# First FFN's down product in four 32-row strips, with weights stationary and x1 kept feature-major

## The reference, cut to what matters

```python
# L0_cond: w = weights[itok_B_1_198];  einsum('bct,bcd->bdt', x, w)
gate_w = spline_reconstruct(gate_cp, 2048, 512)
up_w   = spline_reconstruct(up_cp, 2048, 512)
down_w = spline_reconstruct(down_cp, 512, 2048)
inter  = jax.nn.silu(einsum('bsh,ih->bsi', h, gate_w)) * einsum('bsh,ih->bsi', h, up_w)
ffn    = einsum('bsi,hi->bsh', inter, down_w)
x = x + ffn                                   # x1
x = x + _L1_ffn_ref(_L1_cond_ref(x, ...), ...)  # W + adapter, then router, top 2 of 8 experts
```

## Time and profile before

| | |
|---|---|
| runs before | 1277.27 us median of 3 (1273.51 to 1279.76) |
| profiled execution | span 1274.5 us, from the first to the last instruction; nothing of this execution outside its span was read, and the span is 2.8 us less than the median of the runs |
| busy in the span | TensorE 1161.4 us (91%), weight loads 1073.4 us (84%), VectorE 647.9 us (51%), ScalarE 476.7 us (37%), GpSimd 679.1 us (53%) |
| instructions | 29820 |

### The profile page before, as it was taken

How to read it: one execution, slowest core, us unless ns; L and a number is a source line. 1 busy time by engine, 2 the same in 40 slices (tenths; PEclk the granted TensorE clock), 3 DMA queues, 4 the chain that set the end, 5 groups by cost and what they waited for, 6 DMA issues and landing times. The chain is left out here.

```text
span 1274.5 us, 29820 instructions
## 1 busy us (share of the span) xinstructions
PE 1161.4 (91%) x9814; PEld 1073.4 (84%) x9815; DVE 647.9 (51%) x1223; ACT 476.7 (37%) x1023; POOL 679.1 (53%) x1035
## 2 busy tenths in 40 slices
PE   2579999999999999989999937999999999999995
PEld 1368899999999998878999936999998999899994
DVE  5867777767767677543444432333333333333332
ACT  2355656565666665532323201222222222222221
POOL 4856666666666666620434432555555545555553
PEclk9769999999999999997999967999999999999998
DMA  6044444445555555436736111475747474744443
GB/s 249 10 147 150 174 174 173 175 179 180 188 195 193 191 189 194 141 135 242 258 105 234 68 43 42 75 177 125 209 80 217 76 217 83 208 79 82 77 77 60
DMA packets 75085, 187.07 MB, mean 147 GB/s; under 512 B 12992, under 2 KB 26056, under 8 KB 70704
## 3 DMA queue, kind: packets, MB, share of 16 engines
q1 hardware_dynamic: 49904, 137.09, 30.6%
q0 software_dynamic: 19200, 38.94, 16.5%
q10 hardware_dynamic: 5952, 10.65, 2.3%
HBM read 114.76 MB, written 71.90 MB: 146 GB/s over the span
## 5 line engine op out<-in xcount | busy, mean ns | idle before, releaser
L880 POOL TENSOR_TENSOR in_lo<-inner,in_hi 128x512 fp32r<-128x512 f32 x128 | 168.6, 1317 | 133.4 <-ACT in_hi L1034 133.2
L1577 POOL TENSOR_TENSOR idle<-small 128x1 f32<-128x1 f32 x284 | 93.3, 331 | 196.7 <-DMA out<-result,scatter_at 123.9
L1655 PE MATMUL banks<-slots,zt_hi 128*128 x568 | 190.4, 335 | 4.9 <-DVE zt_lo L1744 2.9
L1657 PE MATMUL banks<-slots,zt_lo 128*128 x568 | 183.8, 324 | 0.0
L1656 PE MATMUL banks<-slots,zt_hi 128*128 x568 | 183.3, 323 | 0.0
L957 PE MATMUL banks<-down_hi,in_hi 64*128 64x320 f32 x1024 | 164.9, 308 | 0.0
L957 PE MATMUL banks<-down_lo,in_hi 64*128 64x320 f32 x1024 | 164.9, 307 | 0.0
L957 PE MATMUL banks<-down_hi,in_lo 64*128 64x320 f32 x1024 | 164.5, 307 | 0.0
L1756 DVE TENSOR_TENSOR hid<-silu_g,banks 128x352 f32<-128x352 f32 x71 | 37.0, 521 | 208.7 <-PE banks L1657 208.7
L1600 POOL DMA_INDIRECT out<-result,scatter_at x71 | 113.7, 1601 | 26.4 <-issue 22.7
L874 POOL TENSOR_TENSOR f_lo<-f_sum,f_hi 128x256 fp32r<-128x256 f32 x128 | 96.3, 769 | 37.8 <-ACT f_hi L1025 34.7
(11 more groups left out here) (221 smaller groups left out, 3055.9 us busy)
## 6 DMA issues: line engine op xcount, KB each, us to landing
gate_up_dram<-split_gu SPq DMA_DIRECT2D x16, 1408.0 KB, 4.9
slots<-gate_up_dram SPq DMA_DIRECT2D x16, 1408.0 KB, 6.8
expert_down_dram<-split_down SPq DMA_DIRECT2D x16, 768.0 KB, 7.1
slots<-expert_down_dram SPq DMA_DIRECT2D x16, 768.0 KB, 7.8
raw_gu<-in_expert_gu SPq DMA_DIRECT2D x16, 704.0 KB, 8.4
x_t<-in_x_t SPq DMA_DIRECT2D x16, 512.0 KB, 3.5
x_both<-in_x SPq DMA_DIRECT2D x16, 512.0 KB, 4.4
x_both<-in_x_res SPq DMA_DIRECT2D x16, 512.0 KB, 3.6
```

What stands on the lines that cost most here:

```text
L880: nc.gpsimd.tensor_tensor(in_lo[:, cs, :], inner[u % 2][:, :, :], in_hi[:, cs, :].bitcast(F32), ALU.subtract).then_inc(in_done, 1)
L1577: nc.gpsimd.tensor_tensor(idle[:, at:at + 1], small[:, 0:1], small[:, 0:1], ALU.add)
L1655: nc.tensor.matmul(psum[bank][:, 0:FD], zt_hi[:, k, :], w_high, start=(k == 0), stop=False)
L1657: ins = nc.tensor.matmul(psum[bank][:, 0:FD], zt_lo[:, k, :], w_high, start=False, stop=(k == DK - 1))
```

## The change

The hidden rows are sorted into 4 classes of 32 rows per group. `down` now takes the weights as the stationary operand (32 rows x 128 columns) and streams 256 tokens; its four classes stand in four 32-row strips of the array, each with a bank of its own. The moment weights become an operand of their own (`mom_w`, 128 columns that hold high and low parts), with two more matmuls. The output is feature-major, so nothing is transposed; `across` runs in three steps over running sums of neighbouring classes. The residual, x1 and its store are feature-major too, so `adapted_layer` loads x1 transposed (into a single buffer), takes high and low parts from SBUF, and makes the token rows of `out` by TensorE's transposes, a ScalarE copy and a store. `features` is 64-row pairs instead of full-array matmuls against a block-diagonal operand. `DOWN_AT` puts the eight `down` products of a tile into six visits. Three of the seven `part` subtractions move from VectorE to GpSimd.

The constants, the new buffer in HBM, and TensorE's products in `prepare`:

```diff
-TURN, CLASSES, DPIECES, DWIN = 128, 2, 16, 20
+TURN, CLASSES, DPIECES, DWIN = 89, 4, 16, 20
...
+        x1t_dram = dram("x1t_dram", [NT, P, DK * TILE])
...
-                    nc.tensor.matmul(bank, own_hi[:, g, :], side_hi[:, :], start=True, stop=False)
-                    nc.tensor.matmul(bank, own_hi[:, g, :], side_lo[:, :], start=False, stop=False)
-                    nc.tensor.matmul(bank, own_lo[:, g, :], side_hi[:, :], start=False, stop=True).then_inc(down_filled, 1)
+                    for a in range(2):
+                        nc.tensor.matmul(bank, own_hi[:, a, g, :], side_hi[:, a, :], start=(a == 0), stop=False)
+                        nc.tensor.matmul(bank, own_hi[:, a, g, :], side_lo[:, a, :], start=False, stop=False)
+                        ins = nc.tensor.matmul(bank, own_lo[:, a, g, :], side_hi[:, a, :], start=False, stop=(a == 1))
```

In `first_ffn` (the visit tables first, then `features`, `down`, `across`, ScalarE's `copy_sums` and VectorE's `body`):

```diff
-        DOWN_AT = {0: [(1, -1, 2), (1, -1, 3), (0, -1, 6)], 1: [(1, -1, 4), (0, -1, 7)], 2: [(1, -1, 5)], 3: [(1, -1, 6)],
-                   4: [(1, -1, 7), (0, 0, 0), (0, 0, 1)], 5: [(0, 0, 2), (0, 0, 3)], 6: [(0, 0, 4)], 7: [(0, 0, 5), (1, 0, 0), (1, 0, 1)]}
-        MOMENTS_AT = {1: 0, 2: 1}
-        TURN_AT, ACROSS_AT = {2: 0, 5: 1}, {3: 0, 6: 1}
-        COPY_AT = {1: 0, 4: 1}
-        FEATURES_AT = {3: [0, 1], 4: [2], 5: [3, 4], 6: [5, 6], 7: [7]}
-        PART_AT = {2: [0, 1], 4: [2, 3], 5: [4], 7: [5, 6]}
+        DOWN_AT = {0: [(-1, 5)], 1: [(-1, 6), (-1, 7)], 4: [(0, 0)], 5: [(0, 1)], 6: [(0, 2), (0, 3)], 7: [(0, 4)]}
+        MOMENTS_AT, SUMS_AT, ACROSS_AT, ADD_AT = 2, 2, 3, 4
+        FEATURES_AT = {0: [(0, 3)], 4: [(1, 0)], 5: [(1, 1)], 7: [(1, 2)]}
+        HIGH_FEATURES_AT = {0: [(0, 2)], 1: [(0, 3)], 5: [(1, 0)], 6: [(1, 1)]}
+        PART_AT = {3: [0], 4: [1], 5: [2, 3], 6: [4, 5], 7: [6]}
...
-                    for s in range(SUB):
-                        to, both = misc_bank[bank][:, s * 2 * P:(s + 1) * 2 * P], pair[:, s, :, :].rearrange("p l n -> p (l n)")
-                        high, low = (f[:, s, 2 * g:2 * g + 2, :].rearrange("p a n -> p (a n)") for f in (feat_hi, feat_lo))
-                        nc.tensor.matmul(to, high, both, start=True, stop=False)
-                        ins = nc.tensor.matmul(to[:, 0:P], low, pair_hi[:, s, :], start=False, stop=True)
+                            for w, feat in enumerate((feat_hi, feat_lo)):
+                                for h in range(2):
+                                    rows = slice(h * SEQ, (h + 1) * SEQ)
+                                    to = view(misc_bank[h], at + s * SEQ, [[P, 2 - w], [1, SEQ]])
+                                    ins = nc.tensor.matmul(to, feat[rows, s, 2 * g:2 * g + 2, :].rearrange("p a n -> p (a n)"), pair[rows, s, 0:2 - w, :],
+                                                           start=(w == 0), stop=(w == 1))
...
-                        for i, (x, w) in enumerate(((in_hi, down_hi), (in_hi, down_lo), (in_lo, down_hi))):
-                            for j in range(CLASSES):
-                                rows = slice(j * NF, (j + 1) * NF)
-                                ins = nc.tensor.matmul(out_bank[s][:, j, 0:NF + CLASS_D], x[rows, c, s * P:(s + 1) * P], w[rows, c, :],
-                                                       start=(c == 0 and i == 0), stop=(c == IC - 1 and i == 2))
+                        for i, (w, x) in enumerate(((down_hi, in_hi), (down_lo, in_hi), (down_hi, in_lo), (mom_w, in_hi), (mom_w, in_lo))):
+                            cols = slice(0, TILE) if i < 3 else slice(TILE, 2 * TILE)
+                            for r in range(CLASSES):
+                                rows = slice(r * ROWS, (r + 1) * ROWS)
+                                ins = nc.tensor.matmul(out_bank[r][:, cols], w[rows, c, :], x[rows, c, :],
+                                                       start=(c == 0 and i == 0), stop=(c == IC - 1 and i in (2, 4)), skip_group_check=True)
...
-                def across(at, t, s):
...
+                def across(t):
+
+                    for step in range(STEPS):
+                        pe.wait_ge(sums_low, STEPS * t + step + 1)
+                        for side, k in ((0, step + 1), (1, STEPS - 1 - step)):
...
+                def copy_sums(t):
+                    act.wait_ge(direct_done, t + 1)
+                    nc.scalar.activation(sums[:, 0, :, :], psum[:, OUT:OUT + CLASSES:CLASSES - 1, TILE:], ACT.Copy).then_inc(sums_copied, 1)
...
                     for v in range(PAIRS):
+                        if v == SUMS_AT and has_last(t):
+                            add_sums(t - 1, 1)
+                            add_sums(t - 1, 2)
+                        if v == MOMENTS_AT + 1 and has_next(t):
+                            low_moments(t + 1, 0)
+                        if v == ADD_AT and has_last(t):
+                            add(t - 1)
                         if has_own(t):
                             multiply(t, v)
...
+                        if v == SUMS_AT and has_last(t):
+                            for step in range(STEPS):
+                                low_sums(t - 1, step)
```

In `adapted_layer`, SyncE's and ScalarE's new steps:

```diff
+                def store_out(t):
+
+                    sp.wait_ge(tok_copied, LSUB * (t + 1))
+                    sp.dma_start(out_tiles[bass.ds(t, 1)].rearrange("a p s h -> p (a s) h"), x1_tok[:, :, :]).then_inc(out_stored, 16)
+
+                def next_x1(t):
+
+                    sp.wait_ge(x1t_low, LSUB * t)
+                    load_x1(sp, t)
...
+                def high(t, b, s):
+                    if s == 0:
+                        act.wait_ge(x1_loaded, 32 * (t + 1))
+                    nc.scalar.activation(x1t_hi[b][:, :, s * P:(s + 1) * P], x1[:, :, s * P:(s + 1) * P], ACT.Copy).then_inc(x1t_high, 1)
+
+                def token_rows(t, s):
...
+                    nc.scalar.activation(x1_tok[:, s, :], psum[bank][:, :], ACT.Copy).then_inc(drained[bank], 1)
```

More of the change, by code:

```diff
@@ L1380, in _ @@
                 for s in range(LSUB):
-                    transpose(0, 0, s)
+                    high(0, 0, s)
+                for s in range(LSUB):
+                    token_rows(0, s)
                 steps(act, body)
```

581 lines of the change are left out of this document (297 added, 284 removed).

## The result

| | before | after |
|---|---|---|
| median of the runs | 1277.07 us (1273.51 to 1279.76, 4 runs) | 1287.31 us (1286.69 to 1290.01, 4 runs) |
| profiled execution, span | 1274.5 us | 1288.3 us |
| busy: TensorE, VectorE, ScalarE, GpSimd | 1161.4, 647.9, 476.7, 679.1 us | 1136.6, 717.9, 507.3, 717.0 us |

The changed kernel takes 1.0084 times the time of the one before (95%: 1.0064 to 1.0103): slower by 0.8%, where 1216 us and a gain were forecast.

What follows compares the result with a forecast made beforehand. TensorE's own stream was taken to bound the FFN tile: 25.9 + 0.6 = 26.5 us. Span 1274.5 - 57 (FFN) - 4 (prepare) - 3 (tail) + 3 (layer) = 1213.5, median 2.8 above the earlier span: 1216 us, range 1193 to 1260.

Steps and rivals of the forecast that it cites:

- TensorE's sum: First FFN, one tile: TensorE's matmuls and shape changes 16.3 us plus 9.6 for down, 25.9 us in all.
- by steps: Rival, down: strips start one after another, 0.15 us a group, tile 28.9 us, kernel 1254 us; chance 0.15.
- as two pairs: Rival, down: only two strips run at once, 0.236 us a group, tile 35.8 us, kernel 1364 us; chance 0.12.
- the walk: Visits 2 to 4 of an FFN tile, followed engine by engine: TensorE waits 0.5 us for VectorE's second multiply.
- the low end: Whole kernel: 0.118 us a group, no stall, shape changes at 0.1 us: tile 25.1 us, kernel 1193 us.
- ends at about 22 us: VectorE's work in one FFN tile after additions and removals, about 22 us, under TensorE's 25.9.
- The rival on VectorE's chain: Rival, FFN visits 2 to 4: three new low parts at 1.3 us each, tile 28.3 us, kernel 1245 us; chance 0.14.
- term of 2.6 us: FFN tile: three subtractions of down weights leave VectorE for GpSimd, 2.6 us off VectorE, 2.0 onto GpSimd.
- clock 1.00: Sign expected in the first FFN: a tile's period of 26.5 us at full clock.
- Prepare and tail: Before the first gate_up, shorter selections, -4 us; after the last gate_up, fewer down visits and the sums, -3 us.
- The layer: Adapted layer: loads into x1's single buffer come late, 0.5 us for six tiles, +3 us (0 to 18).

Runs made afterwards that it cites:

- one_input: Changed kernel with VectorE's four subtractions of expert gate/up weights replaced by reductions with one SBUF operand, low parts left out: 1240.78 us, 0.9656 of the kernel before.
- all_dve: Changed kernel with all seven subtractions of expert weights on VectorE, none on GpSimd: 1254.89 us, 0.9759 of the kernel before.
- after_again: The changed kernel, unaltered, run again on a second chip: 1279.91 us, 0.9936 of the kernel before.
- late_before: The kernel before, with a reduction of 3712 elements on VectorE ahead of one multiply a tile as a delay: 1382.84 us, 1.0740 of the kernel before.
- tuned: all_dve with x1's load ahead of the layer's store, no expert-weight subtraction in visit 3, and a later gather on GpSimd: 1259.27 us, 0.9789 of the kernel before.
- half_loads: FFN of tuned without the gather's wait; each half of x1 loaded once its own readers are done, ahead of the store: 1234.04 us, 0.9659 of the kernel before.
- experts_late: First FFN of half_loads, layer as in the changed kernel, but the first three experts' weights loaded after it: 1245.71 us, 0.9752 of the kernel before.

## Why the prediction was wrong

**TensorE's sum: right.** A group takes 0.12 us, 9.4 for 9.6 us in all. Feature pairs start every 0.11 us (28 steps in 3.1 us), forecast 0.116; across takes 2.6 us, half a microsecond of it waiting, for 2.1. With next to nothing in the way the tile is 26.93 us (one_input) for 26.5 forecast. The rivals on strips, by steps and as two pairs, fell, and with them both estimates from the Trainium skill. By the prediction's estimates the 20 cycles per instruction of the Trainium skill, "Runtime: NRT & Kernel Launch", section Instruction fetch mechanics, would make 0.133 us of eight instructions, and the 3.07 of the Trainium skill, "TensorE: Matmul & The Clock Gate", Part 3, 0.154; measured are 0.117. Two slips of the sum changed nothing: the walk finds 0.5 us of waiting and the tile adds 0.6, and the low end's terms make 24.6 us a tile and not 25.1.

**VectorE: the step that failed.** I wrote that VectorE "ends at about 22 us" and that TensorE waits 0.5 us in visit 4. VectorE has 26.08, and TensorE waits 2.8 us, 1.8 of them for the `multiply` of visit 6. I sized each operation by its median and summed. The row that warned was quoted: L1143 with a maximum of 1634 ns. I used it in the rival on VectorE's chain, for the three new low parts. Of these only the third is slow, and the damage is done by the old subtractions, once GpSimd's run grew by the three operations moved to it. I priced that move as busy time of two engines with room to spare. In the trace of before, one subtraction in each of 14 tiles took about 1.47 us, and ended 0.4 us after the in_lo that GpSimd ran beside it; looking at why would have given the mechanism. My own term of 2.6 us for the three subtractions that move held it too, since three of 256 elements that nothing holds take 1.2:

```profile
L1146 DVE TENSOR_TENSOR split_down<-raw_down,split_down x48: 410/753/2119, 98.3 to 557.8; 128x256 fp32r<-128x256 f32 x48
```

The rule stands in the Trainium skill, "SBUF — State Buffer", section Who interferes with whom: a VectorE instruction with two inputs in SBUF contends with a GpSimd instruction that reads SBUF, one with a single input doesn't. By that rule, one_input agrees (0.52 us in all 64 cases), and 3.88 us against 0.52 is its price here. The page speaks of one instruction that blocks; here VectorE is held over four boundaries between GpSimd's instructions in one place of the tile, and gets in at such a boundary in others.

**The clock: assumed, not argued.** "The tile's period is 26.5 us at clock 1.00" took the clock from the kernel before, in which TensorE hardly idles. With waits of 1.8 us in every tile it fell: 15.9 periods of 29.2 would be 464 us, measured are 481.2, so by this estimate 17 us of the first execution are the clock. all_dve, with waits of at most 0.8 us in its steady tiles, keeps 1.00 in them. The Trainium skill, "TensorE: Matmul & The Clock Gate", section A second HAM failure mode: psum-queue depth-cycling, describes a clock lost to short idles between groups of matmuls. The changed kernel (0.93) and one_input, which loses the waits and has 1.00 in its steady tiles, agree.

**Prepare and tail: right** (-4.7 for -4, -2.4 for -3).

**The layer: right in kind, wrong in size.** I charged 3 us, with 18 as the far end; it is 16.2, and 13.0 on the chip of after_again and late_before. I had seen the release at 12.6 us and the store ahead of the load. I had not seen the expert weights, which the added wait in SyncE's queue moved from before 604 us into the third and fourth tile's loads, nor that the first tile must wait a whole load (5 us), since its buffer is only free when the first products begin.

**The sum.** Of the 60 us missing in the FFN, some 43 are 2.7 us in each of 15.9 tiles and 17 the clock. The rival on VectorE's chain, at 1245 us and 0.14, had the right engine, but priced 1.8 us a tile and no clock.

## What to carry to other kernels

Before a subtraction of two SBUF tiles is put on VectorE beside a busy GpSimd, lay the two queues side by side and look for the longest run of GpSimd without a gap: the subtraction, and all that is queued behind it, can wait until that run ends (3.6 to 4.0 us here). Moving work to an engine with room to spare can therefore cost more than it frees, and where its run breaks matters more than the load. When TensorE's sum falls below what the helpers deliver, count on idle time, and on its clock going with it; and when a double buffer becomes a single one, release it by parts, and look at what else its queue carries in that stretch.

## What was unexpected of the hardware

- A VectorE subtraction of 352 elements from two SBUF operands takes 0.51 to 3.93 us, depending on what GpSimd runs beside it. The same length with one SBUF operand takes 0.52 in all 64 cases.
- The longest waits run over three or four boundaries of GpSimd's unbroken run (ten operations in 8.6 us), to its end, and not to the end of the one operation that they met. Other subtractions of the same tiles get in at a boundary without a gap. It goes the other way too: an in_lo that starts during such a subtraction takes 1.61 us for 1.27.
- The same program had a mean clock of 0.93, 0.95 and 0.97 in its first FFN on three occasions, with 18 us between the first and the last (the last had somewhat shorter waits).
- A group of four 32-row matmuls of 256 columns starts every 0.12 us, no slower than one full-array matmul of that length.
- Where TensorE waited no longer than 0.9 us (all_dve, tuned, half_loads), the clock stayed at 1.00. A single wait of 1.99 us near the end of the stage was followed by a short stretch at 0.50 in one_input, all_dve and half_loads, and by none in tuned and experts_late. With 1.5 to 1.8 us in every tile it fell in some tiles; with 4.26 us in every tile of late_before the mean was 0.92.
- Left open: what decides whether such a wait brings the clock down; what decides whether VectorE gets in between two of GpSimd's operations; and whether a version with fewer low parts in SBUF would bring the tile of 27.2 us to 26.9. A second buffer of x1 was not tried.
